# A cross-attention step issued in another order on five queues, with GpSimd's value copies between two groups of its masks

## The reference

```python
x = x + _L0_attn_ref(_layernorm(x, axis=-1), L0_attn_Wq, L0_attn_Wk)
x = x + _L0_xattn_ref(_layernorm(x, axis=-1), ctx_1024, ctx_1024, ...)
x = x + _L0_ffn_ref(_layernorm(x, axis=-1), ...)

# _L0_xattn_ref, 16 heads of 8 features
scores = jnp.einsum('bhnd,bhmd->bhnm', q, k) * scale
weights = jax.nn.softmax(scores, axis=-1)
out = jnp.einsum('bhnm,bhmd->bhnd', weights, v)
return out.transpose(0, 2, 1, 3).reshape(B, N, EMBED) @ Wo.T
```

## Time and profile before

| what | value |
|---|---|
| median of 3 runs | 507.67 us (506.4 to 509.29) |
| the profiled execution, its own time | 506.03 us |
| its span | 504.2 us |
| granted clock, mean | 0.993 |
| PE, DVE, ACT, POOL busy over the span | 461.2, 413.8, 375.3, 289.0 us |
| cross-attention, steps 0 to 13 | 137.94 to 268.13 us |

### The profile page before, as it was taken

One profiled execution on the slowest core, in us unless ns is written; L12 is line 12 of the kernel. 1 busy time (PEld: TensorE's weight loads), 2 busy tenths in 40 slices (PEclk: granted clock), 3 DMA queues, 4 the chain that ended last, 5 costly groups with the idle time before them and its releaser, 6 DMA issues.

```text
span 504.2 us, 21722 instructions
## 1 busy us (share of the span) xinstructions
PE 461.2 (91%) x8732; PEld 316.9 (63%) x8732; DVE 413.8 (82%) x1118; ACT 375.3 (74%) x563; POOL 289.0 (57%) x380
## 2 busy tenths in 40 slices
PE   3999998999879999999998879999999997899995
PEld 1777776655446666666665556565655555788884
DVE  4788667879688898898887888898988865899995
ACT  3888866888888788788788558888888667655550
POOL 3444223874758768778765756789999842013000
PEclk9999998999999999999999899999999999999999
DMA  6377549630001101111111111223323234277664
GB/s 198 84 181 186 147 124 243 175 108 1 1 25 28 46 27 35 38 27 37 36 27 38 33 43 44 110 88 109 97 100 125 79 121 154 68 223 210 188 181 119
DMA packets 53311, 49.22 MB, mean 98 GB/s; under 512 B 14192, under 2 KB 40944, under 8 KB 53232
## 3 DMA queue, kind: packets, MB, share of 16 engines
q1 hardware_dynamic: 53232, 48.13, 32.8%
HBM read 30.81 MB, written 17.04 MB: 95 GB/s over the span
## 4 chain that ended last, share of the span: by engine, by line
PE 34%; DVE 17%; POOL 15%; issue 5%; ACT 3%; DMA 1%; POOLq 0%; DVEq 0%; SPq 0%; ACTq 0%
DVE c_mx L635 10%; PE ps L1638 6%; PE ps L1557 6%; PE ps L863 3%; POOL v_or_front L1045 3%; PE ps L1461 3%; PE ps L965 3%; PE ps L834 2%; DVE copies_or_layer L626 2%; PE ps L1194 2%; POOL e_inv_root L1074 2%; PE ps L896 2%; POOL e_scaled L1356 2%; POOL e_inv_root L1059 2%; POOL k_or_hidden L1364 2%
## 5 line engine op out<-in xcount | busy, mean ns | idle before, releaser
L635 DVE TENSOR_REDUCE c_mx<-ps 128x16 f32<-128x1024 f32 x64 | 78.0, 1219 | 20.3 <-PE ps L834 20.3
L572 POOL TENSOR_TENSOR copies_or_layer<-k_or_hidden,w_mask 128x512 bf16<-128x512 f32 x80 | 83.5, 1070 | 2.6 <-DVE c_work L666 2.6
L737 ACT ACTIVATE c_work<-ps 128x2048 f32<-128x2048 f32 x32 | 59.9, 1872 | 23.8 <-PE ps L863 23.6
L1530 ACT ACTIVATE copies_or_layer<-k_or_hidden 32x512 f32 (+1 forms) x64 | 40.2, 628 | 24.8 <-PE ps L1557 24.2
L1356 POOL TENSOR_TENSOR e_scaled<-e_raw,e_rden 128x512 f32<-128x512 f32 x16 | 20.8, 1298 | 45.2 <-DMA e_rden<-dispatch_inverses 45.2
L1543 DVE TENSOR_TENSOR o_slot_out<-ps,w_b 128x512 f32<-128x512 f32 x64 | 41.2, 686 | 6.1 <-PE ps L1557 5.6
L1407 ACT ACTIVATE e_slot_in<-ps 128x1024 f32<-128x1024 f32 x30 | 30.7, 1022 | 17.2 <-PE ps L1461 17.2
L747 ACT ACTIVATE c_q_bd<-x_all,w_mask 128x512 f32<-128x512 f32 x64 | 42.7, 719 | 0.0
L592 POOL COPY c_v_bd<-v_or_front 64x512 f32<-64x512 f32 x32 | 21.6, 676 | 30.7 <-PE ps L883 29.4
L1461 PE MATMUL ps<-copies_or_layer,v_or_front 64*128 64x256 f32 x256 | 36.0, 400 | 3.5 <-ACT e_slot_in L1407 3.1
L1638 PE MATMUL ps<-o_slot_out,ctx_sb 128*64 128x129 f32 x512 | 36.8, 282 | 1.4 <-DMA ctx_sb<-combine_scratch 0.9
(11 more groups left out here) (165 smaller groups left out, 1173.7 us busy)
## 6 DMA issues: line engine op xcount, KB each, us to landing
x_all<-x_scratch SPq DMA_DIRECT2D x64, 128.0 KB, 3.2
combine_scratch<-v_or_front SPq DMA_DIRECT2D x16, 512.0 KB, 2.7
ctx_sb<-combine_scratch SPq DMA_DIRECT2D x16, 512.0 KB, 3.3
x_sb<-in_x SPq DMA_DIRECT2D x16, 256.0 KB, 3.2
x_scratch<-a_x SPq DMA_DIRECT2D x16, 256.0 KB, 2.4
ctx_sb<-in_ctx SPq DMA_DIRECT2D x16, 256.0 KB, 3.5
e_rden<-dispatch_inverses SPq DMA_DIRECT2D x64, 64.0 KB, 2.1
out<-o_y SPq DMA_DIRECT2D x32, 128.0 KB, 3.0
```

The lines of the kernel that those rows point to most:

```text
L572: ins = nc.gpsimd.tensor_tensor(k_bd[:, c.m2, s, :], k32[:, c.v, :], w["mask8"][:, s:s + 1].to_broadcast([P, TOK]), ALU.mult)
L635: nc.vector.reduce_max(mx[:, c.m2, :, p], ps[:, SCORE:SCORE + 2, :].rearrange("p a (h m) -> p (a h) m", m=N), AX_X).then_inc(mx_sb.sem, 1)
L737: nc.scalar.activation(prob[:, h, :], ps[:, 0:4, :].rearrange("p a b -> p (a b)"), ACT.Exp, scale=float(HD) ** -0.5).then_inc(p_sb.sem, 1)
L1530: ins = self.nc.scalar.activation(self.h_bd[at, c.m2, :, :, e % 2, :].rearrange("p s g k -> p g s k"), self.hidden[at, :, bass.ts(c.v, SC ...
```

## The change

The work is nearly the same; its order differs on all five queues. On PE the output product of a chunk moves from the end of the step behind to the beginning of the next, behind the first quarter of scores; quarter 1 stands before the transpose of the maxima, quarter 2 directly behind the second half of `scores_T`, and quarter 3 before the transposes of `o_tok`. On DVE the third mask is gone, and mask 0 and the first maximum stand before the sum with x. POOL makes that mask (six in place of five), in two groups of three, and the copies of v stand between the groups. ACT makes the four masked copies of q one by one around the exponentials. The four DMAs of the negated maxima are one DMA with four rows.

```diff
@@ sync
-                for T in range(4):
-                    sp.dma_start(neg_row[32 * T:32 * T + 1, c.m2, :], negmax[16 * T:16 * (T + 1), c.m2, :]).then_inc(max_in.of(c), 16)
+                sp.dma_start(neg_row[0:P:32, c.m2, :], negmax[:, c.m2, :]).then_inc(max_in.of(c), 16)
@@ gpsimd
+        def values_bd(c):
...
+            pool.wait_ge(v_sb.sem, v_sb.at(c))
+            if c.plus(-2): pool.wait_ge(o_ps.sem, o_ps.at(c.plus(-2)))
+            if not c.v: pool.wait_ge(k_bd_pool.sem, k_bd_pool.at(c.plus(2)))
+            elif c.plus(2): pool.wait_ge(k_bd_half.sem, k_bd_half.at(c.plus(-1)))
+            else: pool.wait_ge(k_bd_pool.sem, k_bd_pool.at(end))
...
-                masks_k(t.plus(EARLY), range(MASKS_DVE, MASK_SLOTS))
+                masks_k(t.plus(EARLY), range(MASKS_DVE - 1, MASKS_DVE + 2))
+            values_bd(t.plus(1))
+            if t.k >= 0:
+                masks_k(t.plus(EARLY), range(MASKS_DVE + 2, MASK_SLOTS))
@@ vector
             normalise(t.plus(-1), 0)
+            spread_k(t.plus(EARLY), 0)
+            row_max(t.plus(2), 0)
             c = t.plus(-2)
...
-            spread_k(t.plus(EARLY), 0)
-            row_max(t.plus(2), 0)
             spread_k(t.plus(EARLY), 1)
             row_max(t.plus(2), 1)
-            spread_k(t.plus(EARLY), 2)
+            row_max(t.plus(2), 2)
             normalise(t.plus(-1), 1)
...
-            row_max(t.plus(2), 2)
             row_max(t.plus(2), 3)
@@ scalar
-            if t.k == CHUNKS - 2: spread_q(end, 0)
+            if t.k >= 0: spread_q(t.plus(1), 0, 1)
             exp(t.plus(0), 0)
+            if t.k >= 0: spread_q(t.plus(1), 1, 1)
...
-            if t.k == CHUNKS - 2: spread_q(end, 2)
-            elif t.k >= 0: spread_q(t.plus(1), 0)
+            if t.k >= 0: spread_q(t.plus(1), 2, 1 if t.k < CHUNKS - 2 else 2)
             exp(t.plus(0), 1)
             raw(t.plus(0), 0)
+            if 0 <= t.k < CHUNKS - 2: spread_q(t.plus(1), 3, 1)
```

More of the change, by code:

```diff
@@ L492, in cross_attention @@
     q_lead_sb, q_bd_sb, v_bd_sb = kit.sig("c_q_lead_sb"), kit.sig("c_q_bd_sb"), kit.sig("c_v_bd_sb", 2)
-    k_bd_lead, k_bd_pool = kit.sig("c_k_bd_lead"), kit.sig("c_k_bd_pool")
+    k_bd_lead, k_bd_half, k_bd_pool = kit.sig("c_k_bd_lead"), kit.sig("c_k_bd_half"), kit.sig("c_k_bd_pool")
     x_again = kit.pairs("c_x_again", 2)
@@ L496, in cross_attention @@
     mT_ps, mT_sb = kit.sig("c_mT_ps"), kit.sig("c_mT_sb")
-    max_in = kit.landings("c_max_in", 4)
+    max_in = kit.landings("c_max_in")
     st_ps, p_sb, o_ps = kit.sig("c_st_ps", 2), kit.sig("c_p_sb", 2), kit.sig("c_o_ps", 2)
@@ L557, in _ @@
         pool.wait_ge(ones_set, 3)
+        def values_bd(c):
+            if not c:
+                return
+            pool.wait_ge(v_sb.sem, v_sb.at(c))
[3 more added lines that the diff above has]
+            else: pool.wait_ge(k_bd_pool.sem, k_bd_pool.at(end))
+            for r in range(2):
+                if r: pool.wait_ge(v_bd_sb.sem, v_bd_sb.at(c, 1))
+                at = slice(N * r, N * (r + 1))
+                nc.gpsimd.tensor_copy(v_bd[at, c.m2, :, :, V1 * r:V1 * r + HD],
+                                      v_all[at, c.v * PC:(c.v + 1) * PC, :].rearrange("p a (h d) -> p a h d", d=HD)).then_inc(v_bd_sb.sem, 1)
         def masks_k(c, slots):
@@ L561, in masks_k @@
                 return
-            if not slots or slots[0] == MASKS_DVE:
+            if not slots or slots[0] <= MASKS_DVE:
                 if c.plus(-2): pool.wait_ge(sc_ps.sem, sc_ps.at(c.plus(-2)))
-            if not slots or c.v and slots[0] == MASKS_DVE:
+            if not slots or c.v and slots[0] <= MASKS_DVE:
                 pool.wait_ge(q_sb.sem, q_sb.at(c))
-                if c.v >= EARLY: pool.wait_ge(v_bd_sb.sem, v_bd_sb.at(c.plus(-2)))
+                if c.v >= EARLY: pool.wait_ge(v_bd_sb.sem, v_bd_sb.at(c.plus(-3)))
                 nc.gpsimd.tensor_copy(q_lead[:, c.m2, :], q32[:, c.v, :]).then_inc(q_lead_sb.sem, 1)
@@ L569, in masks_k @@
                 pool.wait_ge(normed.sem, normed.at(end))
+            if c.v >= EARLY and slots[0] > MASKS_DVE: pool.wait_ge(v_bd_sb.sem, v_bd_sb.at(c.plus(-2)))
             for s in slots:
-                if s == MASKS_DVE: pool.wait_ge(k_sb.sem, k_sb.at(c))
+                if s == slots[0] <= MASKS_DVE: pool.wait_ge(k_sb.sem, k_sb.at(c))
                 ins = nc.gpsimd.tensor_tensor(k_bd[:, c.m2, s, :], k32[:, c.v, :], w["mask8"][:, s:s + 1].to_broadcast([P, TOK]), ALU.mult)
                 if s == MASK_SLOTS - 1: ins.then_inc(k_bd_pool.sem, 1)
+                elif s == MASKS_DVE + 1 and c.v >= EARLY: ins.then_inc(k_bd_half.sem, 1)
         for t in steps:
@@ L583, in _ @@
                                         ALU.pow).then_inc(rooted.sem, 1)
[L584 to L593, removed]
             if t.k in EARLY_LEAD:
@@ L626, in spread_k @@
             ins = nc.vector.tensor_scalar(k_bd[:, c.m2, s, :], k32[:, c.v, :], w["mask8"][:, s:s + 1], None, ALU.mult)
-            if s == 2:
+            if s == MASKS_DVE - 2:
                 ins.then_inc(k_bd_lead.sem, 1)
@@ L811, in _ @@
                 nc.scalar.activation(oT[:], ps[:, MISC, :], ACT.Identity, bias=w["bqkv"][:, 2:3]).then_inc(oT_sb.sem, 1)
-            if 0 <= t.k < CHUNKS - 2: spread_q(t.plus(1), 2)
             if t.k == CHUNKS - 1:
@@ L932, in _ @@
             if t.k >= 0: scores(t.plus(2), 0)
+            c = t.plus(-2)
+            if c:
+                pe.wait_ge(oT_sb.sem, oT_sb.at(c))
+                for p in range(PC):
+                    ins = nc.tensor.matmul(ps[:, MISC, p * P:(p + 1) * P], oT[:, p * P:(p + 1) * P], w["woT"][:],
+                                           start=True, stop=True)
+                ins.then_inc(wo_ps.sem, 1)
             values(t.plus(-1), 1)
+            if t.k >= 0: scores(t.plus(2), 1)
             c = at(t, 1)
@@ L938, in _ @@
                 nc.tensor.transpose(ps[0:PC * HEADS, MISC, 0:P], mx[:, c.m2].rearrange("p h a -> p (h a)"), w["ident"][:]).then_inc(mT_ps.sem, 1)
-            if t.k >= 0: scores(t.plus(2), 1)
             scores_T(t.plus(0), 1)
+            if t.k >= 0: scores(t.plus(2), 2)
             turn(t.plus(-1), 1)
-            if t.k >= 0: scores(t.plus(2), 2)
             values(t.plus(0), 0)
@@ L947, in _ @@
                 dispatch.turn_maxima(pe, Chunk(None, 0))
+            if t.k >= 0: scores(t.plus(2), 3)
+            if t.k == CHUNKS - 2: scores_T(end, 0)
             c = t.plus(-1)
@@ L953, in _ @@
                 ins.then_inc(oT_ps.sem, 1)
-            if t.k >= 0: scores(t.plus(2), 3)
-            if t.k == CHUNKS - 2: scores_T(end, 0)
             if t.k == CHUNKS - 1:
@@ L960, in _ @@
             turn(t.plus(0), 0)
[L961 to L967, removed]
             if t.k == CHUNKS - 1: dispatch.logits(pe, Chunk(None, 0))
```

## The result

The changed kernel takes 500.75 us in the median of 6 runs (500.17 to 503.04), the kernel before 506.52 (6 runs): ratio 0.9895, 95% interval 0.9862 to 0.9927, about 1% faster. The profiled execution took 500.89 us. Three sets of rows answer to those of before.

A forecast was written before the change was run, and what follows sets the result against it. PE and VectorE in turn were taken to set the 9.28 us step. Step 0 -0.5, steps 1 to 12 -2.3, step 13 +0.1, tail +1.3: -1.4, 506.03 to 504.6 us, 506.2 as median; range 502.8 to 509.4.

The forecast's parts named there:

- Sum: Whole kernel: -0.5 - 2.3 + 0.1 + 1.3 = -1.4, from 506.03 to 504.6 us in the profile's scale.
- the lift: Whole kernel: median of the runs, 507.67, lies 0.32% above the profiled execution, so 504.6 becomes 506.2 us.
- Steps 1 to 12: Attention stage's steady steps: each goes from 9.28 to 9.09 us, 0.19 less, winning 12 x 0.19 = 2.3 us.
- Bounds: 0.58 [...] and 0.76 [...]. I take the middle: End of a steady step: slot of four transposes before `scores_T`, 0.58 to 0.76 us, giving a step of 9.00 to 9.18.
- So two masks and one normalisation lie on the cycle.: Steady step of the kernel before: VectorE's two masks and one normalisation were read as part of the 9.28 us period.
- Step 0: PE's idle 0.48 us before `scores_T(1,0)`: only one q copy stands behind the raw copy, so 0.5 us won at most.
- Step 13: No masks for VectorE; last maximum stands at 7.86 in place of 7.75, so 0.1 us lost.
- Drain: Tail: chunk 14's output product moves behind the logits' transposes, delaying its sum with x and the last chunk; 1.3 us lost.
- The row goes out in one DMA: zero.: Negated maxima in one DMA and not four: zero in quiet steps, since the transfer is hidden already.
- ScalarE's single copies: Masked q copies one by one around the exponentials: cost zero, the fourth ending near 8.7, 0.4 before it is needed.
- The slower rival: Steady steps: mask 0 blocked by a whole GpSimd mask, 0.43 us a step; 509.8 or 511.4 us; chance 0.13.
- The faster rival: Tail's delay caught up and short transition, 0.28 us a step: 502.1 us, 503.8 in the median's scale; chance 0.37.

The follow-up runs named there:

- GpSimd: Kernel before with only GpSimd's new order (six masks, three on either side of the copies; VectorE two): 505.82 us, ratio 0.9966.
- transfer: Kernel before with the row of negated maxima sent in one transfer and not four, nothing else: 506.02 us, ratio 1.0006.
- ScalarE alone: Kernel before with only ScalarE's new order, masked copies of q one by one: 511.37 us, ratio 1.0118.
- the kernel with the product put back: Changed kernel with chunk 14's output product back ahead of the logits' transposes, run twice: 500.55 and 501.27 us, ratios 0.9865 and 0.9897.
- copies of v first: Changed kernel with GpSimd's copies of the values ahead of both groups of masks: 536.68 us, ratio 1.0595 to the kernel before.

## Why the prediction was wrong

- **Sum.** 504.6 was forecast in the profile's scale, 500.89 came, 3.7 us less. Another 1.6 came from lifting the forecast by 0.32% to a median of three runs; six runs put the median of before at 506.52, 0.1% over its profile. No one term makes the miss of 5.45 us in the median: it is some 1.7 from the slot below, 1.6 from the lift, 1.5 that was not in the sum, and 0.65 from where the stage began.
- **Steps 1 to 12: forecast -2.3, measured -5.5** (112.44 to 106.97 us). The step that failed is "Bounds: 0.58 [...] and 0.76 [...]. I take the middle": the slot of four transposes before `scores_T` is 0.53, so a step wins 0.334 and not 0.19, 4.0 in all. The mechanism of the new step was right: `o_tok` transposes at 7.92, held by the normalisation (PE's loader waits 0.41 there, its matmuls start some 0.2 later than they could), mask 1 at 0.48. That 7.92 came out to the hundredth is partly luck: the product's slot is 1.08 and not 0.99, and maximum 2 starts 0.46 behind its quarter and not 0.53, which cancel.
- **The other 1.5 us of steps 1 to 12 was not in the sum.** Step 1 is 0.70 shorter, 0.37 more than a steady step wins, since chunk 0's product now falls into step 2. And steps 2 and 3 of the kernel before had a pause inside their second 32 score matmuls, 1.48 and 1.75 us for 1.05, at granted clock 1.00. The three kernels with TensorE's old order whose other steps stayed near those of before (GpSimd, transfer, ScalarE alone) show such pauses in steps 2 to 4; none of the six profiles with TensorE's new order and 8.94 us steps has one in steps 2 or 3, though three have one in step 0 or 1. What makes it stays open.
- **"So two masks and one normalisation lie on the cycle."** The sum of 9.28 is right, this reading of it is not: with the third mask off VectorE the step of the kernel before stays 9.28. From quarter 1 the cycle ran over PE (the quarter, `scores_T(t,1)`, the transposes, 196.94 to about 199.16), then the normalisation, maximum 2 and quarter 3. The third mask ended just when those transposes did, and quarter 2 did not wait for the maximum behind the second one. The forecast survived this, since it laid out the new step afresh and credited no mask.
- **Step 0: -0.5 forecast, -0.38 measured** (8.47 to 8.09). **Step 13: +0.1 forecast, +0.11** where the forecast had it, at the last maximum (7.86 into the step and not 7.75). PE's own steps 13 and 14 are 0.34 and 0.42 shorter, but VectorE's moments bound what follows: from the start of step 13 to `scores_T(15,1)` it is 23.19 us, before 23.07. **Drain: +1.3 forecast, +1.11 measured,** and the second profile of the kernel with the product put back has the 16.28 us of before.
- **Not of the change:** the stage began 0.65 us earlier (137.29 against 137.94); over all profiles here it begins between 135.8 and 138.6, in either order. This is luck of the profiled execution and accounts for part of the 3.7. Behind the drain 0.17 was lost.
- **"The row goes out in one DMA: zero."** The net was right, the reason was not: it is zero in the old order and about 9 us in the new. A part of the change that I had costed at nothing was one that the rest could not do without. The same holds for ScalarE's single copies, 28 us, costed at zero with "0.4 before it is needed"; the slack is 0.19.
- **The slower rival** needed a mask that a GpSimd mask holds up. In the changed kernel mask 0 takes 0.48, and GpSimd's three masks beside it 3.27 and not the 3.04 of its other three. With TensorE's old order in the changed kernel it takes 1.05 beside GpSimd's masks, so the effect exists and the phase of the new order avoids it. With the exclusive lock of the Trainium skill (SBUF — State Buffer, "Who interferes with whom") these rows agree in so far as one of the two engines is held up each time; no row here shows VectorE held for a whole GpSimd mask of 1.04, and none of this sets the step.
- **The faster rival** came nearest: it had the slot at 0.58, so 0.28 a step, but took the drain as caught up, which it is not.

## What to carry to other kernels

An order written over several engines is one object: cost an edit that looks free also against the new order, by writing down for each hand-over when it is asked for and when it is needed, and keep those with under 1 us of slack on a list. For a slot that no row shows, a bound from its neighbours isn't a bound; a slot between two other kinds can be shorter than both, so let the range go beyond. And to learn whether an instruction lies on the cycle, take it out: the engine may only wait in its place. A wait of TensorE's can cost more than its length, as with the copies of v first.

## What the runs showed of the hardware

- Requests on SP's queue take about 0.6 us each (2.44 for four, 0.58 for one), and PE went 2.86 us after the last of four. Asking for four small transfers in place of one takes 1.86 us longer.
- The same instructions in the drain had a stretch at TensorE's lower level in one profile (0.71 over four microseconds, after a window with 2.19 of 4.00 us busy) and none in that kernel's second profile. With one product 1 us later the median rose by 4.7 us, and the profile has windows of 0.59 and 0.50, the first of them ahead of that product.
- VectorE's mask takes 0.48 us beside nothing (before, 204.12), 0.81 beside GpSimd's copies, 1.05 and 1.12 beside its masks; in the changed kernel it takes 0.48 beside GpSimd's masks, and those take 0.23 more for three.
- In two kernels `scores_T` starts 0.10 us after ScalarE's last q copy, while the profile puts the wait before it (1.37, 1.61 us) down to "issue".
